# Conditioning jobs moved from two engines to one, and packed into fewer rounds

## What is computed

```
x = x + attention(cond(x, side, side, w1, u1, t), ...)      16 query heads, 4 key/value heads of 128
x = x + experts(cond(x, side, side, w2, u2, t), ...)        64 experts, the best 8 of each token

cond(r, k, v, w, u, t):                                     here k = v = side, and r = x
  tf    = sigmoid(sum(t))
  decay = exp(-exp(w)) * (0.5 + 0.5 * tf)                   one factor per channel
  ek, ekv = exp(min(k, 30)),  ek * v
  nf, df = scan forward:  a = a * decay + ekv,  b = b * decay + ek
  nb, db = the same scans, backward in time
  euk   = exp(min(u + k, 30))
  out   = sigmoid(r) * (nf + nb - ekv + euk * v) / max(df + db - ek + euk, 1e-8) * (0.8 + 0.2 * tf)
```

## Time and profile before

| | |
|---|---|
| median of 3 runs | 774.96 us (774.29 to 778.01) |
| the profiled execution | 773.04 us |
| its span, first to last instruction | 771.3 us |
| start, to the end of the first queries' low half | 0 to 56 us |
| job (0,1) and the first scores | 56 to 86 us |
| the 16 rounds | 86 to 343 us |
| experts | 343 to 771 us |
| busy: PE, DVE, ACT, POOL | 693.0, 475.8, 374.1, 159.2 us |
| mean granted clock of TensorE | 0.952 of full |

### The profile page before, as it was taken

How to read it: one execution, slowest core, us unless ns; L and a number is a source line. 1 busy time by engine, 2 the same in 40 slices (tenths; PEclk the granted TensorE clock), 3 DMA queues, 4 the chain that set the end, 5 groups by cost and what they waited for, 6 DMA issues and landing times.

```text
span 771.3 us, 10244 instructions
## 1 busy us (share of the span) xinstructions
PE 693.0 (90%) x3527; PEld 589.0 (76%) x3527; DVE 475.8 (62%) x947; ACT 374.1 (49%) x864; POOL 159.2 (21%) x124
## 2 busy tenths in 40 slices
PE   3984789898898889869699999999999999999997
PEld 3973678787787788748588888888888888888885
DVE  3837687776878586855455555555555565555554
ACT  6433666756575677562433443434443344334422
POOL 1505010011101110120312332123311332223300
PEclk8687899999999999995899999999999999999999
DMA  9110002001000100300544234433344223442111
GB/s 333 61 37 20 1 1 56 0 1 57 1 1 1 56 1 1 123 1 0 157 144 131 67 117 116 143 92 104 100 133 143 74 96 116 143 125 73 55 55 54
DMA packets 42930, 57.60 MB, mean 75 GB/s; under 512 B 2952, under 2 KB 34960, under 8 KB 42640
## 3 DMA queue, kind: packets, MB, share of 16 engines
q1 hardware_dynamic: 42896, 57.17, 23.7%
HBM read 55.82 MB, written 1.34 MB: 74 GB/s over the span
## 4 chain that ended last, share of the span: by engine, by line
PE 72%; DVE 15%; ACT 8%; DMA 2%; issue 1%; SPq 1%; DVEq 0%; ACTq 0%
PE ps L913 16%; PE ps L915 15%; PE ps L914 15%; PE ps L1108 6%; PE ps L1109 6%; PE ps L1110 6%; PE ps L1050 3%; ACT lg L462 3%; PE ps L917 2%; DVE lg L771 2%; DVE df L704 2%; DMA gw_rows<-n_L_ffn_gate_weight_dram 1%; PE ps L953 1%; DVE ptl L821 1%; ACT lg L530 1%
## 5 line engine op out<-in xcount | busy, mean ns | idle before, releaser
L913 PE MATMUL ps<-h2h,guh 128*128 128x512 f32 x384 | 150.7, 392 | 0.0
L914 PE MATMUL ps<-h2l,guh 128*128 128x512 f32 x384 | 150.3, 391 | 0.0
L915 PE MATMUL ps<-h2h,gul 128*128 128x512 f32 x384 | 150.1, 391 | 0.0
L631 ACT ACTIVATE sact<-ps 128x512 f32<-128x512 f32 x96 | 57.4, 598 | 190.0 <-PE ps L915 190.0
L438 POOL TENSOR_TENSOR gul<-gu_raw,guh 128x384 fp32r<-128x384 f32 x64 | 77.5, 1235 | 274.1 <-ACT guh L462 274.1
L895 DVE TENSOR_TENSOR uact<-ps,wb 128x512 f32<-128x512 f32 x96 | 66.4, 692 | 104.1 <-PE ps L915 99.7
L900 DVE TENSOR_TENSOR al<-aact,ah 128x512 fp32r<-128x512 f32 x96 | 88.4, 920 | 67.6 <-ACT ah L462 67.6
L462 ACT ACTIVATE ah<-aact 128x512 fp32r<-128x512 f32 x96 | 60.7, 633 | 49.3 <-DVE aact L898 34.5
L913 PEld LDWEIGHTS ps<-h2h,guh 128*128 128x128 f32 x384 | 72.8, 190 | 15.2
L914 PEld LDWEIGHTS ps<-h2l,guh 128*128 128x128 f32 x384 | 72.8, 190 | 15.2
L915 PEld LDWEIGHTS ps<-h2h,gul 128*128 128x128 f32 x384 | 72.6, 189 | 15.3
(11 more groups left out here) (173 smaller groups left out, 1266.1 us busy)
## 6 DMA issues: line engine op xcount, KB each, us to landing
gu_raw<-ffn_gate_up_weights_dram SPq DMA_DIRECT2D x16, 768.0 KB, 5.4
wb<-combine_rows SPq DMA_DIRECT2D x30, 384.0 KB, 3.5
wb<-combine_rows SPq DMA_DIRECT2D x30, 256.0 KB, 3.8
dn_raw<-_L_ffn_down_weights_dram SPq DMA_DIRECT2D x16, 384.0 KB, 6.1
wb<-combine_rows SPq DMA_DIRECT2D x34, 128.0 KB, 3.0
wq_raw<-in_L_attn_Wq_dram SPq DMA_DIRECT2D x1, 2048.0 KB, 11.9
wo_sb<-in_L_attn_Wo_dram SPq DMA_DIRECT2D x1, 2048.0 KB, 14.9
bm<-bias_rows SPq DMA_DIRECT2D x4, 512.0 KB, 3.5
```

Of the source, the lines that this page charges most:

```text
L913: nc.tensor.matmul(o_, a[0], b_[0], start=start, stop=False)
L914: nc.tensor.matmul(o_, a[0], b_[1], start=False, stop=False)
L915: return nc.tensor.matmul(o_, a[1], b_[0], start=False, stop=stop)
```

## The change

GpSimd takes no part in the jobs any more: its products and sums become VectorE instructions. The clamps at 30 move behind the exponential (the bound is then exp(30)), so that u is added as ScalarE's bias and euk is read straight from vT, by two activations of 128 x 256 instead of one of 128 x 512. The exponentials of the keys, `ek`, and the products `ekv` are taken by job (0, b) and kept for job (1, b) in two alternating buffers; a job (1, b) therefore has no part 0, and its last multiplication moves into part 3. The backward scan reads one step on and has its two operations exchanged (`add` of the next element, then `mult` by the decay), so that what it writes is already without its own term, and one addition of 128 x 512 replaces two `scalar_tensor_tensor` of 128 x 256. The order of the jobs changes; 22 parts are dealt out instead of 30. `hf` has one buffer instead of two. The masks and the low halves of the weights stay on GpSimd, and what stood between them there is gone.

```
-        jobs = [(0, 0), (0, 1), (0, 2), (1, 0), (0, 3), (1, 1), (1, 2), (1, 3)]
+        jobs = [(0, 0), (0, 1), (1, 0), (0, 2), (1, 1), (0, 3), (1, 2), (1, 3)]
-        round_jobs = [(c, b, part) for c, b in jobs[2:] for part in range(PARTS)]
+        round_jobs = [(c, b, part) for c, b in jobs[2:] for part in (range(PARTS) if c == 0 else range(1, 4))]
...
-            cond_products((0, 0))
             pool.wait_ge(wkv_hi, 1)
             nc.gpsimd.tensor_tensor(wkl[:], ...).then_inc(wkv_lo, 1)
-            cond_sums((0, 0))
             pool.wait_ge(wkv_hi, 2)
             nc.gpsimd.tensor_tensor(wvl[:], ...).then_inc(wkv_lo, 1)
             wq_low(0)
             wq_low(1)
-            cond_products((0, 1))
             masks(0)
-            cond_sums((0, 1))
             wq_low(2)
             wq_low(3)
...
             def cond_exps(job):
-                act.wait_ge(cond_in, job_no[job] + 1)
-                nc.scalar.activation(ek[:], ek[:], ACT.Exp)
-                nc.scalar.activation(euk[:], euk[:], ACT.Exp).then_inc(cond_exp, 1)
+                c, b = job
+                n = job_no[job]
+                if n:
+                    act.wait_ge(cond_left, n)
+                if c == 0:
+                    act.wait_ge(cond_in, b + 1)
+                    nc.scalar.activation(ek[b % 2][:, :, 0:T], ek[b % 2][:, :, 0:T], ACT.Exp)
+                for cc in range(CC):
+                    ins = nc.scalar.activation(euk[:, cc, :], vT[:, cc, b * T:(b + 1) * T], ACT.Exp,
+                                               bias=wu[:, 4 * c + 2 + cc:4 * c + 3 + cc])
+                ins.then_inc(cond_exp, 1)
...
-                    if part == 0:
+                    if part == c:
                         cond_exps((c, jb))
...   cond_part on VectorE, its new body:
+                def both_ways(fore, x):
+                    for cc in range(CC):
+                        V.tensor_tensor_scan(out=fore[:, cc, :], data0=d(cc), data1=x[:, cc, 0:T], initial=0.0, op0=ALU.mult, op1=ALU.add)
+                        ins = V.tensor_tensor_scan(out=rev(back[:, cc, :]), data0=rev(x[:, cc, 1:T + 1]), data1=d(cc), initial=0.0,
+                                                   op0=ALU.add, op1=ALU.mult)
+                    link(ins)
+                    return V.tensor_tensor(fore[:], fore[:], back[:], ALU.add)
                 if part == 0:
+                    V.tensor_scalar(ek_[:, :, 0:T], v, EXP_CAP, None, ALU.min).then_inc(cond_in, 1)
                 elif part == 1:
+                    if c == 0:
+                        dve.wait_ge(cond_exp, n + 1)
+                        link(V.tensor_tensor(ekv_[:, :, 0:T], ek_[:, :, 0:T], v, ALU.mult))
+                    link(both_ways(nf, ekv_))
+                elif part == 2:
+                    both_ways(df, ek_)
                     dve.wait_ge(cond_exp, n + 1)
+                    link(V.scalar_tensor_tensor(out=eukv[:], in0=euk[:], scalar=EXP_OF_CAP, in1=v, op0=ALU.min, op1=ALU.mult))
                 elif part == 3:
+                    V.scalar_tensor_tensor(out=df[:], in0=euk[:], scalar=EXP_OF_CAP, in1=df[:], op0=ALU.min, op1=ALU.add).then_inc(cond_left, 1)
+                    dve.wait_ge(cond_left, n + 1)
+                    V.tensor_tensor(nf[:], nf[:], eukv[:], ALU.add)
                     link(V.tensor_scalar(df[:], df[:], 1e-8, None, ALU.max))
                     link(V.reciprocal(df[:], df[:]))
+                if part == 3 and c == 1:
+                    link(V.scalar_tensor_tensor(out=sig[:, :, b * T:(b + 1) * T], in0=nf[:], scalar=ofac[:, b:b + 1], in1=df[:], op0=ALU.mult, op1=ALU.mult))
+                if part == 4:
+                    link(V.scalar_tensor_tensor(out=nf[:], in0=nf[:], scalar=ofac[:, b:b + 1], in1=df[:], op0=ALU.mult, op1=ALU.mult))
+                    dve.wait_ge(turned_act, 4)
+                    if b:
+                        dve.wait_ge(proj_hi, order[("G", b - 1, 0)] + 1)
+                        dve.wait_ge(h_hi, b)
+                    V.tensor_tensor(hf[:], nf[:], sig[:, :, b * T:(b + 1) * T], ALU.mult).then_inc(h_full, 1)
```

More of the change, by code:

```diff
@@ L102, in adaln_attn_ffn @@
         wd_sb = tiny("wd_sb", [P, KV, KV])
-        ek = at("ek", [P, CC, T], take(2 * KIB))
-        ekv = at("ekv", [P, CC, T], take(2 * KIB))
+        ek = [at(f"ek{i}", [P, CC, T + 8], take(CC * (T + 8) * 4)) for i in range(2)]
+        ekv = [at(f"ekv{i}", [P, CC, T + 8], take(CC * (T + 8) * 4)) for i in range(2)]
         euk = at("euk", [P, CC, T], take(2 * KIB))
@@ L109, in adaln_attn_ffn @@
         df = at("df", [P, CC, T], take(2 * KIB))
-        nb_ = at("nbk", [P, CC, T + 8], take(CC * (T + 8) * 4))
-        db_ = at("dbk", [P, CC, T + 8], take(CC * (T + 8) * 4))
-        hf = at("hf", [P, 2, CC, T], take(4 * KIB))
+        back = at("back", [P, CC, T], take(2 * KIB))
+        hf = at("hf", [P, CC, T], take(2 * KIB))
         hh = at("hh", [P, 2, CC, T], take(4 * KIB), F32R)
@@ L379, in f32 @@
                 return a.bitcast(F32)
[L381 to L392, removed]
             def masks(b):
@@ L673, in cond_part @@
                 v = vT[:, :, b * T:(b + 1) * T]
-                d = lambda cc: decay[:, c, cc, b:b + 1]
-                if part == 0:
[L677 to L681, removed]
-                elif part == 1:
-                    dve.wait_ge(cond_exp, n + 1)
[L684 to L698, removed]
-                        ins = V.scalar_tensor_tensor(out=df[:, cc, :], in0=db_[:, cc, 1:T + 1], scalar=d(cc), in1=df[:, cc, :], op0=ALU.mult, op1=ALU.add)
-                    ins.then_inc(cond_scan, 1)
@@ new lines, in cond_part @@
+                d = lambda cc: decay[:, c, cc, b:b + 1].to_broadcast([P, T])
+                ek_, ekv_ = ek[b % 2], ekv[b % 2]
+                def both_ways(fore, x):
[5 more added lines that the diff above has]
+                    return V.tensor_tensor(fore[:], fore[:], back[:], ALU.add)
@@ L779, in row_sums @@
                 V.reciprocal(rinv[:, u % 2, :], rsum[:, u % 2, :]).then_inc(recips, 1)
-            V.memset(nb_[:, :, T:T + 8], 0.0)
-            link(V.memset(db_[:, :, T:T + 8], 0.0))
+            for i in range(2):
+                V.memset(ek[i][:, :, T:T + 8], 0.0)
+                ins = V.memset(ekv[i][:, :, T:T + 8], 0.0)
+            link(ins)
             for k in (0, 1):
@@ L973, in proj @@
                         for cc in range(CC):
[L974 removed]
+                            ins = nc.tensor.matmul(p[:, t * 2 * KV:(t + 1) * 2 * KV], hf[:, cc, t * P:(t + 1) * P], wgd[:, cc, :],
                                                    start=(cc == 0), stop=(cc == CC - 1))
```

24 lines of the change are left out of this document (4 added, 20 removed).

## The result

The changed kernel takes 794.48 us (median of 4 runs, 793.55 to 795.06), the kernel before 775.55 us beside it: a ratio of 1.0239 [1.0211, 1.0267]. It is slower, as forecast, and 8.5 us above the 786 predicted. The profiled span grew from 771.3 to 791.1 us, +19.8, and the mean granted clock fell from 0.952 to 0.932.

A forecast was written before the change was run, and what follows sets the result against it. The experts' stage was taken as bound by TensorE, with VectorE the path in stretches before it. 773.04 + 1.2 + 5.0 + 2.1 + 3.0 = 784.3, with the median 1.9 above: 786 predicted, range 776 to 796.

The forecast's parts named there:

- The rows that were named as signs: Profile rows expected, such as wql 2 and 3 directly after the masks and round 0 logits near 72 us.
- The clock: Rounds: TensorE's granted clock falls after its waits, three falls of 1.0 us, +3.
- rival 1: Rounds: the clock falls in most of them, +14 us instead of +3, giving 797; chance 0.17.
- the −8.1: Rounds 11 to 13: with no parts left they run at the floor, 39.4 us against 47.5.
- The rounds' terms: Rounds: lengths summed from early and late parts; rounds 1 to 10 take 182.2 us against 172.7, +9.5.
- Rival 3: Rounds 1 to 10: the packed parts hide and these stay at 172.7; 774 us by the median; chance 0.09.
- The start: Before G: low halves hold VectorE's scans, hf comes 2.3 us later and G, behind hh and wgd, 1.2.
- Job (0,1): Before the rounds: wql 2 and 3 land on scans and additions, part 3 is 1.35 longer; +5.0 us.
- rival 2: Start and job (0,1): VectorE wins the port and GpSimd waits; 777 us by the median; chance 0.17.
- rival 4: Backward scans: the exchanged form is slow, 1.2 us each, +14, 798; or at 0.40, −4, 782; chance 0.05.
- rival 3 with rival 2's free port: Rounds and port: packed parts hide and VectorE also wins the port; 769 us, no separate chance given.

The follow-up runs named there:

- e2: Changed kernel with 7 to 12 idle TensorE products ahead of its waits for ql in eight rounds; 784.32 us.
- e1: Changed kernel with one more wait: GpSimd starts wql 2 and 3 only when the logits of round 0 are made; 790.14 us.
- c1: Kernel before with 5 to 8 idle TensorE products ahead of the wait for ql in rounds 3, 6, 11 and 13; 771.63 us.
- e10: Changed kernel with one more wait: GpSimd takes wvl, then wql 0 and 1, only when hf of job (0,0) is written; 796.38 us.
- e5: Changed kernel with the idle products of e2 and the wait of e1 together; 779.85 us.
- e3: Changed kernel with the product euk * v and both sums back on GpSimd and the clamp at exp(30) left out; 782.85 us.
- e6: Changed kernel with VectorE's jobs cut into short steps dealt by length and GpSimd's low halves held until VectorE is not scanning; 773.65 us.
- e11: e6 with earlier round 0 logits, a third ek/ekv buffer pair, the old job order, more even dealing, idle products and eukv on back; 763.94 us.

## Why the prediction was right, and where its sizes were off

**The sign and the mechanisms** held: VectorE is not relieved, GpSimd's low halves land on its scans, the packed rounds give back less than they cost. The rows that were named as signs came: `wql` 2 and 3 at 63.55, logits of round 0 at 71.4 (about 72 forecast), rounds 12 and 13 of 13.13, round 10 of 18.0 (18.1), rounds 3 and 7 of 17.7 and 17.6 (16 or more), free backward scans of 0.66. One did not: round 11 took 14.6, not 13.1, for the clock.

**The clock: the term that was mis-sized.** Forecast were 3.0 us for three falls of 1.0; there were seven falls worth 10 us in rounds 1 to 10 (e2), 1.4 each, and one of 1.5 in round 11. That was rival 1 (eight falls), which I held at 0.17; its price of 1.8 a fall was too high, so the result, 794.5, lies between the forecast and its 797. The reason for counting so few was that round 11 of before had the same gap as round 13 and kept the clock. That was worked out from the terms, and the trace of before does not bear it out: TensorE waited 1.54 us for `ql` in round 11 and 1.93 in round 13. The gaps forecast for the changed kernel were too short as well: 1.6 for rounds 2 and 6 leaves out the 0.4 for ScalarE's exponentials that the same prediction adds to those rounds (6.09 + 3.87 + 0.4 − 8.24 = 2.1). Measured waits are 2.16 and 2.08 there, 2.74 and 2.66 in rounds 3 and 7, 2.86, 2.85 and 2.86 in rounds 1, 5 and 9, and all seven fell; rounds 4 and 8, with an early part of 3.17, and round 10, with a wait of 1.28, kept the clock. The length of the wait alone does not decide it: 1.53 us went before the fall in round 6 of before, and 1.54 in rounds 3 and 11 before none; 2.85 in round 9 of e1 before none. (The fall in round 13 of before lasted from 315.6 to 319.0 us, less than the 5 of the prediction.)

With 10 + 1.5 in place of 3 the sum would be 794.5. That this is just what was measured is in part luck: the end of round 0 came 6.0 us later and not 6.9, rounds 1 to 10 were 1.0 over their terms, and the median lies 0.9 above the profiled execution where it lay 1.9 above it before. The execution of before from which the sum starts had lost 2 to 3 us in the same way (c1); the fall of its round 13 went with that round's part and stands in the −8.1.

**The rounds' terms.** Rounds 1 to 10: 182.2 forecast, 183.2 measured at full clock (e2). Single rounds of e2 agree as well: 19.6 against 19.4 (rounds 1 and 5), 16.7 against 16.4 (2 and 6), 16.05 against 16.2 (3 and 7), 19.74 against 19.7 (4 and 8), 21.0 against 20.7 (9), 18.07 against 18.1 (10). Rival 3 (the parts hide) is out: it had these rounds at 172.7.

**The start.** +1.2 forecast through hf, hh and `wgd`. Four instructions were held as described, but hf was only 1.7 us later, not 2.3, and e10 shows that its way is not what ends last: freeing it moved G by 0.12 us. G was 0.5 later, as TensorE's own products were, and the low half of the first queries was done 1.2 us later. The other 0.7 goes with the clock, which was at 0.50 until 48.5 us where it had been until 45.9; that it is the cause is argued and not shown. The size agreed by chance; the step was wrong.

**Job (0,1).** +5.0 forecast, 3.7 of it ahead of the logits of round 0 and 1.35 in part 3. Without the 1.2 that came along from the start, the logits were 3.3 later and hf 4.4. The held scans alone, priced at 4.7, are worth 4.0 to 4.2 (e1, e5): each of the two subtractions makes one scan longer by 2.1 us. And from the logits to hf it took 18.37 us instead of 17.29, 1.1 more.

**Who wins the port** (rival 2: GpSimd waits). It is out: in e1 the same scans without a GpSimd partner took 0.66. The rows at 64.04 and 66.74 show the two engines alternate: one scan waits for one subtraction, and then the next for the next. The Trainium skill ("SBUF — State Buffer", Who interferes with whom) says that the first to issue keeps the port for its whole instruction; the rows agree, a scan beside a subtraction of 128x1024 taking 2.77 us instead of 0.66. That VectorE, with its next instruction always ready, gets the port in between just once is what the rows add.

For instructions with a single input in SBUF the prediction left out a condition: the Trainium skill ("SBUF — State Buffer", Who interferes with whom) says that they do not contend outside the modes that use both ports. This clamp of the kernel before has one such input and stood beside `wvl` (29.91 to 32.26); whether it ran in such a mode no row shows, but it was held; free, it takes 0.42:

```profile
29.99 2.55 DVE L703 TENSOR_SCALAR df<-df 128x512 f32<-128x512 f32 x1 [2.61 <-POOL df L392]
```

**The exchanged scan** (rival 4) is priced at 667 ns in e3, like the other: neither 0.4 nor 1.2 apart. What the prediction concluded from the Trainium skill ("DVE: opcode table, instruction layouts, handler registers and perf-mode slots", Datapath and trigger behaviour), that the exchanged form costs the same as the built-in one, agrees. Two sums of the prediction were slightly off: 798 for this rival should have been 800 (786 + 14), and rival 3 with rival 2's free port 768 and not 769.

## What to carry to other kernels

Before work is moved from an idle engine to a busier one, ask in which wait of the third engine it will lie: in the plain rounds here every microsecond by which an early part grew was one more of TensorE's waiting, and a fall of the clock behind such a wait cost 1.4 us more on average. Work that sits ahead of something awaited is best cut into short steps and dealt by their length, no piece longer than the slack of its place; dealt so, and with GpSimd's low halves kept off the scans, the same arithmetic went from 2.4% slower to level with the kernel before (e6, ratio 0.9981). A third pair of buffers, earlier logits and idle products made it 1.4% faster (e11). Removing an engine's work also removes the order that it imposed on what comes behind it: look at what runs earlier, and against what.

## What the runs showed of the hardware that I had not expected

Idle products shortened the kernel by 10.2 us: TensorE doing more was faster. A gain ahead of a stage can be taken back by the clock in one execution and kept in another: e1's profiled execution brought hf 4.3 us forward and ended round 0 only 1.5 earlier; e5's, with the same instructions up to there, brought hf 4.1 forward and ended it 3.6 earlier. A vector instruction with two inputs in SBUF that met a GpSimd subtraction was held whatever its kind: scans (2.79), a `scalar_tensor_tensor` of 128x512 (2.86), and in e3 an addition (2.65).
